# Ten tables looked up by matmul, and each chunk's dense layers right behind its pair products

## The reference

```python
e = jnp.stack([tbl_f[ids[:, f]] for f in range(27)], axis=1)      # 512 x 27 x 128
inter = jnp.einsum('bfd,bgd->bfg', e, e)                          # pair products
x = inter.reshape(512, 27 * 27)[:, TRIL_IDX]                      # the 351 pairs with j < i
h = jnp.concatenate([r_bottom, x, r_bottom], axis=1)              # 128 + 351 + 128 = 607
h = jnp.maximum(h @ W_top1 + b_top1, 0.0)                         # 607 -> 512
h = jnp.maximum(h @ W_top2 + b_top2, 0.0)                         # 512 -> 256
y = h @ W_top3                                                    # 256 -> 1
```

## Time and profile before

| | |
|---|---|
| median of 3 runs | 121.84 us (120.61 to 122.99) |
| the profiled execution | 119.64 us |
| its span, first to last instruction | 117.5 us |
| PE busy | 92.8 us, 79% |
| DVE busy | 74.8 us, 64% |
| ACT busy | 63.7 us, 54% |
| POOL busy | 72.8 us, 62% |

### The profile page before, as it was taken

How to read it: one execution, slowest core, us unless ns; L and a number is a source line. 1 busy time by engine, 2 the same in 40 slices (tenths; PEclk the granted TensorE clock), 3 DMA queues, 4 the chain that set the end, 5 groups by cost and what they waited for, 6 DMA issues and landing times.

```text
span 117.5 us, 3583 instructions
## 1 busy us (share of the span) xinstructions
PE 92.8 (79%) x1464; PEld 77.8 (66%) x1464; DVE 74.8 (64%) x230; ACT 63.7 (54%) x150; POOL 72.8 (62%) x75
## 2 busy tenths in 40 slices
PE   6608999999899999794458399955899838992992
PEld 6503788878688788583357299843798718980990
DVE  5418899999999999864994062164154656793001
ACT  7525698997996985563162162361165506990010
POOL 2777777777777787777777777677677620001000
PEclk9999999999999999999999967999999999999689
DMA  3749999999999767793112212113122220000000
GB/s 39 164 132 261 252 248 237 242 244 247 230 242 234 179 165 214 290 300 92 46 45 76 62 50 67 50 50 86 49 59 59 58 58 6 0 6 21 0 0 1
DMA packets 7347, 14.28 MB, mean 121 GB/s; under 512 B 2149, under 2 KB 4485, under 8 KB 7332
## 3 DMA queue, kind: packets, MB, share of 16 engines
q1 hardware_dynamic: 5104, 9.58, 32.8%
q0 software_dynamic: 2208, 4.47, 14.5%
q10 hardware_dynamic: 20, 0.01, 0.1%
HBM read 13.81 MB, written 0.00 MB: 118 GB/s over the span
## 4 chain that ended last, share of the span: by engine, by line
POOL 59%; issue 18%; PE 10%; DMA 6%; DVE 3%; ACTq 1%; DVEq 0%
POOL rows L309 59%; PE pH L587 5%; DMA rows<-in_tbl,ids_sb 3%; DVE Z L342 3%; PE pT L587 2%; PE pG L613 2%; DMA ids_sb<-in_ids 2%; DMA Z<-Z 1%; PE pF L538 1%; ACTq L247 1%; PE pT L527 1%; DVE prod L484 0%; DVE ET L321 0%; DVEq L129 0%
## 5 line engine op out<-in xcount | busy, mean ns | idle before, releaser
L309 POOL DMA_INDIRECT rows<-in_tbl,ids_sb x68 | 71.6, 1054 | 21.6 <-issue 20.4
L465 DVE TENSOR_SCALAR hot<-ids_b,row_f 125x512 fp32r<-125x512 int16 (+1 forms) x75 | 31.8, 452 | 1.7 <-DMA ids_b<-in_ids_t 1.7
L342 DVE COPY Z<-pG 26x96 f32<-26x96 f32 (+1 forms) x80 | 19.5, 244 | 19.5 <-PE pG L613 18.5
L342 ACT COPY Z<-pG 26x96 f32<-26x96 f32 (+1 forms) x80 | 18.7, 234 | 16.3 <-PE pG L613 15.4
L563 PE MATMUL pG<-hot,high 125*128 125x512 f32 x72 | 22.0, 422 | 4.7 <-ACT high L352 4.2
L563 PE MATMUL pG<-hot,low 125*128 125x512 f32 x72 | 20.2, 404 | 0.0
L462 DVE TENSOR_TENSOR low<-tbl,high 125x256 fp32r<-125x256 f32 x44 | 18.2, 414 | 3.1 <-ACT high L352 3.1
L563 PEld LDWEIGHTS pG<-hot,high 125*128 125x128 f32 x72 | 13.6, 196 | 9.3 <-ACT high L352 4.5
L613 PE MATMUL pG<-ET 128*26 128x26 f32 x1024 | 13.5, 194 | 7.1 <-issue 4.6
L613 PEld LDWEIGHTS pG<-ET 128*26 128x26 f32 x1024 | 11.2, 104 | 10.1 <-issue 7.9
L563 PEld LDWEIGHTS pG<-hot,low 125*128 125x128 f32 x72 | 14.1, 196 | 3.1
(11 more groups left out here) (39 smaller groups left out, 57.6 us busy)
## 6 DMA issues: line engine op xcount, KB each, us to landing
tbl<-in_tbl SPq DMA_DIRECT2D x11, 448.0 KB
ids_b<-in_ids_t SPq DMA_DIRECT2D x9, 128.0 KB, 5.2
rows<-in_tbl,ids_sb POOLq DMA_INDIRECT x68, 5.0
W1Z<-in_w_tiles SPq DMA_DIRECT2D x1, 768.0 KB
tbl<-in_tbl SPq DMA_DIRECT2D x11, 52.0 KB
W1A_B<-in_w_ab SPq DMA_DIRECT2D x1, 512.0 KB, 3.8
W2S<-in_W_top SPq DMA_DIRECT2D x1, 512.0 KB
botT<-in_bottom_t SPq DMA_DIRECT2D x1, 256.0 KB, 4.0
```

The costliest lines, as they stand in the source:

```text
L309: pool.indirect_dma_start(out=rows[:, c % 2, slot[f], :], out_offset=None, in_=tables[f][:, :], in_offset=bass.IndirectOffsetOnAxis(ap=ids ...
L342: last = engine_copy(to[:, :, STAGE - n:STAGE, :, s, :], of)
L465: nc.vector.tensor_scalar(hot[0:TP, n % 2, k, columns(n)], ids_b[0:TP, n % TABLE_RING, columns(n)], row_f[0:TP, k:k + 1], None, ALU.is_equ ...
```

## The change

The tables that are looked up for all samples become ten. The tables that the plan picks change with it: two are still late, chunks 0 and 1 have runs of 2, 4, 2, 1, 4 and 4 tables, chunk 2 of 2, 4, 2, 1, 1, 2 and 3, and chunk 3 splits its last one into 2 and 1. That makes 17 + 17 + 15 + 15 = 64 gathers, and 12 instead of 11 tables through the ring.

The first table is loaded and rounded in two halves, and the second table's load no longer waits for the first ids. VectorE makes all of its `hot` blocks before the parts of `low`, and TensorE takes all `high` matmuls before the `low` ones. The number of warm-up matmuls goes from 34 to 72. The weights' loads lose their two waits on SyncE. Both late tables are prepared ahead of chunk 0's moves. A chunk's units follow each other without runs between them. Chunk 2's dense layers move ahead of chunk 3's last four runs, out of the middle of its units.

```diff
-N_ONE_HOT = 9
+N_ONE_HOT = 10
-WARM_UP = (20, 14)
+WARM_UP = 72
@@ SyncE
-                elif n:
-                    sp.wait_ge(ids_b_in[n - 1], 16)
-                sp.dma_start(tbl[0:TP16, n % TABLE_RING, :, :], t[0:TP16, :, :]).then_inc(tbl_in[n], 16)
-                sp.dma_start(tbl[TP16:TP, n % TABLE_RING, :, :], t[TP16:TP, :, :]).then_inc(tbl_in[n], 16)
-            sp.wait_ge(tbl_in[N_ALL - 1], 32)
+                for x in range(pieces(n)):
+                    ks = slice(x * TABLE_K // pieces(n), (x + 1) * TABLE_K // pieces(n))
+                    landed = tbl_half_in if x + 1 < pieces(n) else tbl_in[n]
+                    sp.dma_start(tbl[0:TP16, n % TABLE_RING, ks, :], t[0:TP16, ks, :]).then_inc(landed, 16)
+                    sp.dma_start(tbl[TP16:TP, n % TABLE_RING, ks, :], t[TP16:TP, ks, :]).then_inc(landed, 16)
             sp.dma_start(W1A_B[:, :, :], w1_ab).then_inc(w1ab_in, 16)
-            sp.wait_ge(w1ab_in, 16)
@@ VectorE
             prepare(N_ONE_HOT)
+            prepare(N_ONE_HOT + 1)
             for c in range(LAST):
-                first, *others = units_of(c)
-                move_gram(nc.vector.tensor_copy, dve, first, 0, z_dve)
-                runs_of(c + 1, 0, BETWEEN[c])
+                for k in units_of(c):
+                    move_gram(nc.vector.tensor_copy, dve, k, 0, z_dve)
+                runs_of(c + 1, 0, 2)
                 if c == 0:
-                    prepare(N_ONE_HOT + 1)
...
+                runs_of(c + 1, 2, 4)
                 if c:
                     dense3(c - 1)
-                runs_of(c + 1, RUNS[c + 1] - LATE_RUNS[c + 1], RUNS[c + 1])
+                if c + 1 == LAST:
+                    dense3(c)
+                runs_of(c + 1, 4, RUNS[c + 1])
@@ TensorE
+            def dense_layer1_pairs(c):
+                wait_packed(c)
+                if c == 0:
+                    pe.wait_ge(ones_done, 1)
+                    pe.wait_ge(w1z_in, 16)
+                for t in range(TILES):
+                    done = pair_tile(c, t)
+                done.then_inc(dense1, 1)
...
+                for k in units_of(c):
+                    gram_unit(k)
+                next_run()
+                next_run()
                 if c == 0:
                     look_up(N_ONE_HOT)
+                    next_run()
+                    look_up(N_ONE_HOT + 1)
+                    next_run()
+                    dense_layer1_bottom(c)
                 else:
+                    dense_layer1_pairs(c - 1)
+                    next_run()
+                    dense_layer2(c - 1)
+                if c + 1 < LAST:
+                    while len(waiting):
+                        next_run()
+                    if c:
+                        dense_layer1_bottom(c)
+                else:
                     dense_layer1_bottom(c)
+                    dense_layer1_pairs(c)
+                    next_run()
+                    dense_layer2(c)
+                    while len(waiting):
+                        next_run()
...
             for k in units_of(LAST):
-                if k == AFTER_DENSE1:
-                    wait_packed(LAST - 1)
-                    for t in range(TILES):
-                        done = pair_tile(LAST - 1, t)
-                    done.then_inc(dense1, 1)
                 gram_unit(k)
-            dense_layer2(LAST - 1)
             dense_layer1_bottom(LAST)
```

More of the change, by code:

```diff
@@ L116, in dlrm_tower_kernel @@
     RUNS = [len(runs[c]) for c in range(CHUNKS)]
-    LATE_RUNS = [2 * (c == LAST) for c in range(CHUNKS)]
-    BETWEEN = [3, 2, 0]
-    AFTER_DENSE1 = UNITS_BY[LAST] - 2
     EARLY_RUNS = min(N_ONE_HOT - 1, RUNS[0])
@@ L200, in dlrm_tower_kernel @@
         z_dve = sem("z_dve")
-        packed = sem("packed")
+        packed = [sem(f"packed_{c}") for c in range(CHUNKS)]
         packed_pool = sem("packed_pool")
@@ L233, in unit_before, with pieces @@
             return max((j for j in range(k) if gram_units[j][3] < at + n and at < gram_units[j][3] + gram_units[j][2]), default=None)
+        def pieces(n):
+            return 1 + (n == 0)
         def columns(n):
@@ L347, in make_high @@
             def make_high(n):
-                act.wait_ge(tbl_in[n], 32)
                 if n >= 2:
                     act.wait_ge(looked_up, n - 1)
-                nc.scalar.copy(high[0:TP, n % 2, :, :], tbl[0:TP, n % TABLE_RING, :, :]).then_inc(high_done, 1)
+                for x in range(pieces(n)):
+                    ks = slice(x * TABLE_K // pieces(n), (x + 1) * TABLE_K // pieces(n))
+                    act.wait_ge(tbl_half_in if x + 1 < pieces(n) else tbl_in[n], 32)
+                    nc.scalar.copy(high[0:TP, n % 2, ks, :], tbl[0:TP, n % TABLE_RING, ks, :]).then_inc(high_done, 1)
             def one_hot_blocks(n):
@@ L457, in prepare @@
                 for k in range(TABLE_K - act_blocks[n]):
[L458 to L463 removed]
                     nc.vector.tensor_scalar(hot[0:TP, n % 2, k, columns(n)], ids_b[0:TP, n % TABLE_RING, columns(n)],
                                             row_f[0:TP, k:k + 1], None, ALU.is_equal).then_inc(hot_done, 1)
+                for at in (slice(k, k + step) for k in range(0, TABLE_K, step)):
+                    dve.wait_ge(high_done, n + 1 + (n > 0 or at.stop > TABLE_K // 2))
+                    nc.vector.tensor_tensor(low[0:TP, n % 2, at, :], tbl[0:TP, n % TABLE_RING, at, :],
+                                            high[0:TP, n % 2, at, :], ALU.subtract).then_inc(low_done, 1)
             for n in range(N_ONE_HOT):
@@ L543, in _ @@
             pe.wait_ge(warm_done, 1)
-            for x in range(sum(WARM_UP)):
+            for x in range(WARM_UP):
                 nc.tensor.matmul(pF[:, 0:P], warm[:, :], warm[:, :], start=True, stop=True)
@@ L550, in look_up @@
                     pe.wait_ge(lookup_moved, n)
-                half = TABLE_K // 2
-                first, second = range(half), range(half, TABLE_K)
-                for x, (part, blocks) in enumerate(((high, first), (low, first), (high, second), (low, second))):
-                    if x == 0:
-                        pe.wait_ge(high_done, n + 1)
-                    for k in blocks:
+                for part in (high, low):
+                    for k in range(TABLE_K):
+                        if part is high and k % (TABLE_K // 2) == 0:
+                            pe.wait_ge(high_done, n + 1 + (n > 0 or k > 0))
                         if part is high and k < TABLE_K - act_blocks[n]:
@@ L564, in look_up @@
                                                 hot[0:TP, n % 2, k, columns(n)],
-                                                start=x == 0 and k == 0, stop=x == 3 and k == TABLE_K - 1)
+                                                start=part is high and k == 0, stop=part is low and k == TABLE_K - 1)
                 last.then_inc(looked_up, 1)
@@ L633, in _, with next_run @@
                     pe.wait_ge(mover(i), moved_until(c, i))
-                waiting = list(range(RUNS[c + 1] - LATE_RUNS[c + 1]))
-                def next_run(until):
-                    if waiting and waiting[0] < until:
-                        transpose_run(c + 1, waiting.pop(0))
-                first, *others = units_of(c)
-                gram_unit(first)
-                next_run(BETWEEN[c])
+                waiting = list(range(RUNS[c + 1]))
+                def next_run():
+                    transpose_run(c + 1, waiting.pop(0))
@@ L657, in _ @@
-                while waiting and waiting[0] < BETWEEN[c]:
-                    next_run(BETWEEN[c])
-                for k in others:
-                    gram_unit(k)
-                next_run(len(RUNS) * P)
-                if c == 0:
-                    dense_layer1_bottom(c)
-                    look_up(N_ONE_HOT + 1)
-                next_run(len(RUNS) * P)
-                if c:
-                    dense_layer2(c - 1)
-                if c + 1 == LAST:
-                    dense_layer1_bottom(c)
```

58 lines of the change are left out of this document (17 added, 41 removed).

## The result

The changed kernel takes **132.22 us** (median of 4 runs, 131.3 to 133.05). The kernel before takes 121.22 in the same comparison (4 runs, 120.29 to 122.99). The ratio is 1.093, 95% interval 1.081 to 1.106: slower, and outside the range of 117.5 to 126.0. The profiled execution of after took 133.05 us, its span is 131.2.

A forecast was written before the change was run, and what follows sets the result against it. GpSimd's gathers were taken as the bound, with the other engines' chain close behind. Span 117.5 + 1.0 (later units) - 0.57 (idle gone) + 0.2 (clock) = 118.1, 120.3 with surroundings, median 122.4 us; range 117.5 to 126.0.

The forecast's parts named there:

- The gathers: GpSimd's stream: four fewer gathers at 1.251 us each, last one starting at 88.9, offering 5.0 us.
- VectorE in the lookups: VectorE's table work: first table done at 10.0, gaining 0 to 2.9 us, taken whole; late tables done at 53.5.
- Second late table: End of VectorE's work on the late tables, both ahead of chunk 0's moves: 3.7 us each, done at 53.5.
- The chain through chunks 1 to 3: TensorE and VectorE handovers: units of chunk 1 at 64.0, chunk 2 at 76.6, chunk 3 at 95.9 without stalls.
- the forecast of 98.3: Start of chunk 3's units: 95.9 plus 2.4 of stalls, 1.0 us later than before.
- Chunk 2's layers: Moved ahead of chunk 3's units: 0.57 us of idle in VectorE's last moves goes, nothing more is saved.
- the gathers' floor: Chunk 3's units could start at 92.3 by the rows alone; the engines put them at 95.9.
- +0.2: Tail: TensorE's lower clock after some 6 us of idle, bounds nothing to +1 us.
- Stalls inside a unit: TensorE's units: 0 to 1.43 us each, mean 0.7, four on the path, 2.4 us after cover by VectorE's moves.
- Rival (2): Units back to back use up fetched instructions, each stalling 1.4 us: span 121.9, median 126.2; chance 0.16.
- Rival (1): Few stalls and overlapping waits: median 119.8 down to 116.2, taken at 118.3; chance 0.28.
- Rival (3): Second table's load delays the first table, VectorE starting up to 2.9 us later: 125.3, half of it 123.9; chance 0.13.

The follow-up runs named there:

- c2: Changed kernel with VectorE's low parts put back between the hot blocks, all tables but the first; 126.66 us, ratio 1.045.
- c1: Changed kernel as it is, run again beside the follow-up experiments; 132.03 us, kernel before 121.30.
- f2: d1 with the units of a chunk side by side again; 153.08 us, ratio 0.961 to the kernel before.
- f1: Changed kernel with only chunk 2's pairs and second layer back in the middle of the last chunk's units; 158.77 us, ratio 1.004.
- d1: c4 with chunk 2's pairs and second layer moved back among chunk 3's units; 115.89 us, ratio 0.969.
- g1: d1's own kernel once more, on the slower kind of chip; 154.32 us, kernel before 160.34.
- f3: d1 with the hot blocks of a table in a row again; 162.78 us, ratio 1.023.
- f4: d1 with both waits in front of the weights' loads; 153.83 us, kernel before 158.93.
- c4: c2 with a chunk's units kept apart by two runs of the next chunk, chunk 3's bottom part between its second and third unit; 124.78 us, ratio 1.037.
- g2: f2's kernel once more, beside g1; 153.52 us, ratio 0.964.
- d3: Kernel before with the early start alone (first table in halves, second load not held back, 72 warm-up matmuls); 120.39 us, ratio 1.003.
- e2: Changed kernel with both waits in front of the weights' loads put back; 167.24 us, ratio 1.028.
- e3: Changed kernel with low parts interleaved again and the weights' two waits put back; 160.90 us, ratio 0.995.
- e4: Kernel before with one edit: VectorE makes all hot blocks of a table before its four low parts; 164.79 us, ratio 1.020.
- e1: Same kernel as c2, on the slower kind of chip; 162.91 us, ratio 0.995.

## Why the prediction was wrong

**The gathers: the step that failed.** "During the loads a gather takes longer ... which I price at 0 to +1 us on the 91.3. It is covered if the engines come later than that." The last gather started at 101.43, not at 88.9, and the delay was not covered: chunk 0's last gather started at 36.48, and TensorE's wait for its rows, 5.59 us, is a term that the sum does not have. The rows that asked for it were all there: one gather in 1.25 us past the lookups, 1.5 during them. I put the difference down to the loads. It is VectorE's work (1.12 to 1.33 us for a gather beside interleaved blocks in c2, 0.94 to 0.95 in after's 7 us without VectorE, with the loads still running), and the change regroups just this work. The regrouping I costed in the part on VectorE as pure gain, 2.9 us. Measured, it costs 5.4 (c1 to c2) and 5.7 (f2 to f1).

**VectorE in the lookups.** First table done: predicted 10.0, measured 11.1. The work is right (4.2 us in after for 4.1), and no `high` was waited for. The start was 6.99 instead of 5.94. Over all profiles it is 5.30, 5.94 and 6.18 in the three kernels that hold the second table's load back, and in the others 5.02 to 5.19 five times and 6.61 to 7.36 twelve times. Both values occur for one kernel (d1 5.02, g1 6.72) and on one chip (f3 5.07, f4 6.63). What decides between them is open. Second late table: predicted 53.5, measured 62.3. Of the 8.8, 1.05 is that start, 7.01 the stand, and the rest small. With the blocks interleaved it is 56.7 (c2); the start there was 7.02, and three waits for `high` of 0.66, 0.16 and 0.52, which I had at nothing, are most of what is left.

**The chain through chunks 1 to 3 held.** From the end of the first run's move to chunk 1's units I had 5.6 us and it took 5.1 (67.26 to 72.37). From there to chunk 2's, 12.6 and up to 1.4 of stall: 14.2. To chunk 3's, 19.3 without stalls; 22.3, with 0.59 and 2.35 of stall in chunk 2's units. The sum was right in its form and began 8.8 us late. Chunk 3's units came 10.5 us behind the forecast of 98.3: those 8.8, and the rest mostly stalls that were priced too low.

**Chunk 2's layers.** "So moving them ahead saves nothing more" was right, and the 3.6 us over the gathers' floor (95.9 against 92.3) were seen: the stage from chunk 2's to chunk 3's units is 3.7 longer in c4 than in d1. The two numbers measure different things, so their agreement does not prove the sum. But I forecast the move as part of a kernel equal to before, and did not see that it is a loss which could be had back by one edit. Its second half I had at +0.2: "I take +0.2, since the pairs were already at the low level." The tail grew by 2.2 instead (20.2 to 22.4), and by 3.4 between d1 and c4. Two stalls of 2.35 and 2.37 us stand in it in after, and the last pairs were granted 0.50 where before had a mixed 0.61. How much of either is due to the layers' place is not shown, since g1 has the 0.50 with the layers where before has them.

**Stalls inside a unit.** 2.4 us on the path was the forecast. Up to chunk 3's units, 1.32, 1.11, 0.59 and 2.35 are in the trace, of which the last three, 4.05, are on the path, with chunk 3's own 2.35 and 2.37 on top, where I had counted none. So this term was too small as well: 2.4 against 4.05, and nothing against up to 4.7 in the tail. Rival (2) had this size, but its mechanism, units back to back, did not show: f2 against f4 and g2 against g1 have no cost. Rival (1) had the time of d1 (115.9), for a kernel that is not the changed one. Rival (3), that the second load delays the first table, is not borne out in the size of 2.9 us: after's first table did not wait for `high`, and d3 has that load unheld and starts at 5.10. A part of it, the late starts of 6.61 to 7.36, is not ruled out.

The rule of the Trainium skill ("Runtime: NRT & Kernel Launch", Instruction fetch mechanics) that instruction fetch is mostly hidden, which I weighed, is not settled by these runs. The stalls are far from hidden in size (4.3 to 10.8 us of "issue" in the changed kernel and its kin on one kind of chip, 24.7 to 40.4 on the other), but no row ties them to the fetch.

**Open.** What makes TensorE stand inside the units, in steps of 0.70 us, and why it differs so between chips. Why it stands more with the `hot` blocks in a row (f3 beside f4, 41.6 and 33.9 us; e2 beside e3, 42.0 and 37.9). Which row holds a gather longer, that of the blocks or that of the parts, and when. Whether c4's splitting of the units is worth anything on the first kind of chip.

## What to carry to other kernels

Where GpSimd issues gathers, the order on VectorE is part of the gathers' price: before grouping its instructions into long rows of one kind, look at how long a gather takes beside them as they are, and beside an idle VectorE. A delay of the issuer shows as a smaller share of it on the chain, so compare the mean of one gather too. Work of the chunk before that stands in the middle of the last chunk's units looks like an obstacle there, but it fills TensorE's waits; moved ahead, it delays the last rows. And before a clock level is put down to an edit, look at a second profile of the same kernel.

## What the runs showed that I had not expected

- A gather of 64 KB is issued in 0.94 us beside an idle VectorE, in 1.12 to 1.33 beside interleaved compares and subtractions (c2, 21 to 30 us), and in up to 4.61 (e4) where four subtractions and a row of six to eight compares follow each other, ending 0.11 to 0.12 us behind the row. Other gathers beside such rows take 1.28.
- The kernel before has a median of 120.4 to 121.3 us on some chips and of 158.9 to 162.4 on others. Most of the difference lies in the 1024 small matmuls: d1's kernel has 5.8 us of idle and 13.2 of work there on one chip, 33.3 and 20.1 on the other (g1), 34.4 of the 38.0 us between the two spans. In the trace of e1 they stand in steps of 0.70 us.
- Dense layers put ahead of the last rows cost 3.7 us up to the last chunk's units (c4 against d1). Behind them the two traces differ by a further 3.4, about half of it the granted clock, which for the same kernel came out at either level (d1 and g1).
